# Expert blocks of a decoder layer: down products in two series, the expert's number read once in mid-block

## The chip, the cores and the metric

The kernel runs on one core of a Trainium2 chip. TensorE (PE in the profile) multiplies, VectorE (DVE), ScalarE (ACT) and GpSimd (POOL) work on what it leaves, and SyncE (SP) starts most of the transfers. The metric is the device time of one execution in microseconds (us); less is better.

## What is computed

The program is one decoder layer over 16 sequences of 128 tokens with 256 channels: a two-way recurrent mix, a cross attention, and a causal attention followed by a mixture of eight experts, each with a layer norm behind it. The change lies in the experts alone. Their part of the reference, cut to what matters:

```python
logits = hn @ w_gate.T
probs = jax.nn.softmax(logits, axis=-1)
tv, ti = jax.lax.top_k(probs, TOPK)          # TOPK = 2 of E = 8 experts
tv = tv / jnp.sum(tv, axis=-1, keepdims=True)
rw = jnp.zeros((T, E), hn.dtype).at[jnp.arange(T)[:, None], ti].set(tv)
for e in range(E):                           # FFN = 896, D = 256
    up = jax.nn.silu(hn @ qgroup(w1[e]).T) * (hn @ qgroup(w3[e]).T)
    moe = moe + rw[:, e:e + 1] * (up @ qgroup(w2[e]).T)
```

`qgroup` rounds weights to 16 levels in groups of 128.

## The kernel before

All stages are written out by hand for each engine; order is the order of the code, and semaphores are the only links between the engines. The last large stage, `experts_stage`, takes the 2048 tokens' two choices each, sorted by expert, in 39 blocks of 128 rows. A block belongs to one expert, whose number stands in a table in memory (`k.block_expert`). Three steps are unrolled at the start (`in_steps`), then a loop of 17 turns with two steps each, then two unrolled steps. Buffers come in pairs: `j` is the block's parity, `n` its number.

One block's way through the engines:

1. GpSimd gathers its rows by an indirect DMA (L2211), three bf16 parts of 256 channels.
2. TensorE turns them with six transposes (`turn`, L2062) into a bank of the accumulator memory (PSUM).
3. ScalarE copies the turned rows out into `expert_parts` (`take_rows`, L2125) and raises `parts_ready`. All products of the block read that tile.
4. For each of seven chunks `f` of the 896 hidden channels TensorE makes an up product of twelve bf16 matmuls (`up_product`, L2074) into one of four banks. ScalarE copies half of it out (`first_chunk`, L2130), VectorE adds the other half twice (`second_chunk`, L2168, `gate_ready`), ScalarE takes the silu (`soften`, L2134), and VectorE multiplies (`multiply`, L2175, `up_ready`).
5. For each chunk TensorE adds a down product (`down_product`, L2084): one f32 matmul of 256 columns in the code, which is two matmuls in the trace. A block's down products are made during the step of the next block.
6. ScalarE scales the sum by the tokens' shares (`take_y`, L2140), and GpSimd adds it to the rows in memory by an indirect DMA (`scatter`, L2239).

In a step TensorE reads two expert numbers with `value_load` (L2066), waits for `parts_ready`, and then alternates: up product `f` of this block, down product `f` of the block behind. After the third pair it turns the next block. ScalarE goes through the chunks in a fixed order: copy `f`, then silu `f-1`; the next block's turned rows are copied after the silu that follows copy 4, and the block behind is scaled after the last silu. An up product waits for `gate_ready` of the product four before it (the first two of an odd block: two before), since there are four banks.

Of the kernel before, what the change touches and what calls it, by code (L numbers as in the profile page):

```python
# [38 lines left out]
E, FFN = 8, 896  # L39
FC = FFN // P  # L40
# [7 lines left out]
BLOCKS = (2 * TOK + E * (ROWS - 1)) // ROWS  # L48
# [14 lines left out]
class Steps:  # L63
# [12 lines left out]
    def turn(self, i, per):  # L76
        self.base, self.at = self.start + i * per, 0
# [1905 lines left out]
def experts_stage(k):  # L1983
# [39 lines left out]
    def in_steps(emit, eng, st=None, per=None):  # L2023

        emit(0, 0, 0, False, 2)
        for j in (1, 0):
            emit(j, 2 - j, 0, True, 2)
        if st:
            st.done(1, st.at)
        with eng.Fori(0, TURNS - 2) as i:  # L2030
            if st:
                st.turn(i, per)
            for j in (1, 0):
                emit(j, 2 * i + 4 - j, i + 1, True, 2)
        if st:
            st.done(TURNS - 2, per)
        emit(1, BLOCKS - 2, TURNS - 1, True, 1)
        emit(0, BLOCKS - 1, TURNS - 1, True, 0)

    def bank(j, f):  # L2040

        g = FC * (1 - j) + f
        return UP + g % 4, 2 if g < 2 else 4

    def slot(j, f):

        return (FC * (1 - j) + f) % 2

    def halves(at):
        return banks[:, at, :].rearrange("p (m c s) -> p m c s", m=2, c=DC)  # L2050

    def turned(j):
        return banks.bitcast(BF16)[:, TURN + j, 0:3 * D]
# [4 lines left out]
    def tensor(pe):  # L2058
        def turn(j, n, i):
            pe.wait_ge(rows_in[j], 16 * i + 16)  # L2060
            for a in range(3 * DC):
                last = pe.transpose(turned(j)[:, a * P:(a + 1) * P], rows[j][:, a, :], k.ident16[:, :])  # L2062
            last.then_inc(block_turned, 1)

        def expert_of(n):
            return pe.value_load(k.block_expert[0:1, bass.ds(n, 1)], min_val=0, max_val=E - 1)  # L2066

        def up_product(j, n, f, expert):
            at, before = bank(j, f)
            pe.wait_ge(gate_ready, FC * n + f + 1 + AHEAD - before)  # L2070
            for m in range(2):
                for c in range(DC):
                    for a in range(3):
                        last = pe.matmul(  # L2074
                            banks[:, at, (m * DC + c) * ROWS:(m * DC + c + 1) * ROWS],
                            levels[:, bass.ds(expert * (2 * JOB) + (m * JOB + (f * DC + c) * P), P)],
                            parts[j][:, a, c, :], start=(a == 0), stop=(a == 2))
            last.then_inc(up_summed, 1)

        def down_product(j, n, f, expert):  # L2080
            if f == 0:
                pe.wait_ge(y_ready, n + 1)
            pe.wait_ge(up_ready, FC * n + f + 1)
            last = pe.matmul(banks[:, Y + j, 0:D], up[j][:, f, :], down[:, bass.ds(expert * JOB + f * D, D)],  # L2084
                             start=(f == 0), stop=(f == FC - 1))
            if f == FC - 1:
                last.then_inc(y_summed, 1)

        def step(j, n, i, prev, more):
            expert = expert_of(n)  # L2090
            last_expert = expert_of(n - 1) if prev else None
            pe.wait_ge(parts_ready, n + 1)
            for f in range(FC):
                up_product(j, n, f, expert)
                if prev:
                    down_product(1 - j, n - 1, f, last_expert)
                if more and f == 2:
                    turn(1 - j, n + 1, i + 1 if prev else 0)
            if not prev:
                sum_shares()  # L2100

        def sum_shares():
            for m in range(2):
                pe.wait_ge(shares_hit, m + 1)
                for b in range(B):
                    last = pe.matmul(OF_SHARE, k.row_hit[:, m, b, :], share_hit[:, m, b, :, :].rearrange("p a b -> p (a b)"),
                                     start=(m == 0 and b == 0), stop=(m == 1 and b == B - 1))
            last.then_inc(shares_summed, 1)

        levels = k.levels[:, :, :].rearrange("p m a -> p (m a)")  # L2110
        down = k.down[:, :, :].rearrange("p m a -> p (m a)")
        pe.wait_ge(k.blocks_ready, 1)
        pe.wait_ge(k.bank_read, BANKS_JOB * (NUMBERS + 1))
        pe.wait_ge(k.expert_loads, 16 * (WHOLES + E - LATE))
        turn(0, 0, 0)
        in_steps(step, pe)
        expert = expert_of(BLOCKS - 1)
        for f in range(FC):
            down_product(0, BLOCKS - 1, f, expert)

    def scalar(act):
        def take_rows(j, n):

            act.wait_ge(block_turned, n + 1)
            act.copy(parts[j][:, :, :, :].rearrange("p a c s -> p (a c s)"), turned(j)).then_inc(parts_ready, 1)  # L2125

        def first_chunk(j, n, f):
            act.wait_ge(up_summed, FC * n + f + 1)
            at, _ = bank(j, f)
            act.copy(chunk[slot(j, f)][:, :, :], halves(at)[:, :, 0, :]).then_inc(chunk_ready, 1)  # L2130

        def soften(j, n, f):
            act.wait_ge(gate_ready, FC * n + f + 1 + AHEAD)
            act.activation(silu[slot(j, f)][:, :], gate[slot(j, f)][:, 0, :], ACT.Silu,  # L2134
                           scale=steps[j][:, 0, 0, f:f + 1]).then_inc(silu_ready, 1)

        def take_y(j, n):
            act.wait_ge(y_summed, n + 1)
            act.wait_ge(target_ready, n + 1)
            act.activation(y[j][:, :], banks[:, Y + j, 0:D], ACT.Copy, scale=share[j][:, :]).then_inc(y_ready, 1)  # L2140

        def step(j, n, i, prev, more):
            act.wait_ge(steps_ready, n + 1)
            for f in range(FC):
                first_chunk(j, n, f)
                if f:
                    soften(j, n, f - 1)
                if more and f == 4:
                    take_rows(1 - j, n + 1)
            soften(j, n, FC - 1)  # L2150
            if prev:
                take_y(1 - j, n - 1)

        act.wait_ge(k.tokens_ready, 2)
        act.wait_ge(k.expert_loads, 16 * (WHOLES + E - LATE))
        act.sem_inc(y_ready, 2)
        take_rows(0, 0)
        in_steps(step, act)
        take_y(0, BLOCKS - 1)

# [40 lines left out]
    def gpsimd(pool):  # L2201
# [66 lines left out]
        scatter(0, BLOCKS - 1, TURNS)  # L2268

    return sync, tensor, vector, scalar, gpsimd  # L2270

# [199 lines left out]
```

## Time and profile before

| | us |
|---|---|
| median of 3 runs | 1233.48 (1231.79 to 1234.1) |
| the profiled execution, device time | 1234.32 |
| span of its trace | 1232.6 |
| busy in it: PE, DVE, ACT, POOL | 992.5, 955.7, 747.3, 603.2 |
| expert blocks, first up product to last down product | 860.7 to about 1203.6 |

Times in the trace count from the span's start. The view of line groups gives the number and mean duration of each kind; the timeline gives starts, from which the distance between two operations of one engine is read. A matmul's duration holds its way through the array, so neighbours overlap in it: the distance from start to start is what it costs in a series.

### The profile page before, as it was taken

The numbers are of one execution on the slowest core, as the hardware profiler recorded it, in microseconds if no ns is written. First come the engines' busy times: TensorE is split into PE (matmuls) and PEld (weight loads), VectorE is DVE, ScalarE is ACT, GpSimd is POOL, SyncE is SP. The second block draws the span as 40 slices with busy tenths as digits, with TensorE's granted clock in tenths as the row PEclk, the third lists the DMA queues.
The fourth block names the chain that finished last, engine by engine and source line by source line (L and its number), as shares of the span: only waits on it lengthen the run. The fifth ranks groups of instructions, "written<-read, shape, count | busy, mean of one in ns | idle before, by whom it ended". The sixth has DMA issues, their size and how long they took to land.

```text
span 1232.6 us, 24890 instructions
## 1 busy us (share of the span) xinstructions
PE 992.5 (81%) x7366; PEld 740.9 (60%) x7367; DVE 955.7 (78%) x2172; ACT 747.3 (61%) x1885; POOL 603.2 (49%) x639
## 2 busy tenths in 40 slices
PE   0486866536989998968999999972999999999990
PEld 0342433325767777745566666652888888888880
DVE  6739999997888888737999988746777767776773
ACT  5844434405888888814667776541666666666663
POOL 2839776853444444411566767542434343333333
PEclk9878888867998999968999999995999999999996
DMA  5850010131333333124122222110112121212124
GB/s 200 336 201 0 1 35 0 34 111 57 113 115 121 124 130 132 52 87 199 54 80 69 69 69 69 61 56 24 31 38 39 36 43 32 43 32 43 32 31 145
DMA packets 53493, 96.77 MB, mean 79 GB/s; under 512 B 9840, under 2 KB 41584, under 8 KB 52928
## 3 DMA queue, kind: packets, MB, share of 16 engines
q1 hardware_dynamic: 45328, 83.35, 19.5%
q0 software_dynamic: 8112, 12.78, 5.9%
q8 instruction: 25, 0.41, 0.1%
q14 instruction: 28, 0.23, 0.1%
HBM read 66.37 MB, written 29.74 MB: 78 GB/s over the span
## 4 chain that ended last, share of the span: by engine, by line
PE 45%; DVE 33%; issue 10%; POOL 5%; ACT 3%; DMA 2%; DVEq 0%; ACTq 0%; POOLq 0%; SPq 0%
PE banks L2074 15%; PE banks L2084 10%; DVE mix_sums L651 4%; DVE carry L638 2%; DVE peak L1131 2%; DVE carry L641 2%; DVE whole_stat L234 2%; PE banks L1378 2%; DVE probs L1134 2%; DVE whole_stat L235 2%; PE banks L1356 2%; PE banks L885 1%; PE banks L1393 1%; PE banks L1401 1%; PE banks L911 1%
## 5 line engine op out<-in xcount | busy, mean ns | idle before, releaser
L2168 DVE SCALAR_TENSOR_TENSOR expert_gate<-banks,expert_steps,expert_chunk 128x128 f32<-128x128 f32 x546 | 165.0, 346 | 97.9 <-ACT expert_chunk L2130 90.0
L2074 PE MATMUL banks<-expert_parts,levels 128*128 128x128 bf16 x3276 | 228.5, 220 | 7.1 <-issue 6.0
L2074 PEld LDWEIGHTS banks<-expert_parts,levels 128*128 x3276 | 202.4, 98 | 47.8 <-issue 20.1
L2084 PE MATMUL banks<-down,up 128*128 x546 | 176.2, 406 | 0.0
L2130 ACT COPY expert_chunk<-banks 128x256 f32<-128x256 f32 x273 | 101.7, 373 | 97.7 <-PE banks L2074 94.0
L2239 POOL DMA_INDIRECT summed_d<-expert_y,expert_target x39 | 62.5, 1604 | 178.6 <-ACT expert_y L2140 175.6
L499 PE MATMUL banks<-x_turned,w_rkv 128*128 128x512 f32 (+1 forms) x192 | 101.6, 689 | 39.4 <-DVE weight L632 38.9
L2134 ACT ACTIVATE silu<-expert_gate,expert_steps 128x128 f32<-128x128 f32 x273 | 110.7, 406 | 21.8 <-DVE expert_gate L2168 19.8
L1100 POOL TENSOR_TENSOR whole<-whole_level,whole_stat 128x896 bf16<-128x896 f32 x32 | 53.3, 1686 | 101.6 <-DVE whole_level L1171 101.6
L2175 DVE SCALAR_TENSOR_TENSOR up<-expert_gate,expert_steps,silu 128x128 f32<-128x128 f32 x273 | 94.8, 347 | 8.2 <-ACT silu L2134 8.2
L499 PEld LDWEIGHTS banks<-x_turned,w_rkv 128*128 128x128 f32 x192 | 41.7, 223 | 97.0 <-issue 96.0
L1028 ACT ACTIVATE whole_level<-whole_raw,whole_stat 128x128 f32<-128x128 f32 x224 | 91.3, 486 | 0.2 <-DVE whole_stat L255 0.2
L2084 PEld LDWEIGHTS banks<-down,up 128*128 128x128 f32 x546 | 83.0, 191 | 0.4
L923 PE MATMUL banks<-v_ones,probs_t 128*128 128x17 f32 x512 | 63.4, 266 | 0.0
L923 PEld LDWEIGHTS banks<-v_ones,probs_t 128*128 128x128 f32 x512 | 62.0, 198 | 0.0
L550 ACT ACTIVATE weight<-weight 128x1024 f32<-128x1024 f32 x16 | 16.9, 1058 | 71.9 <-DVE weight L632 71.9
L393 PE MATMUL banks<-consts,level 128*128 128x128 f32 x84 | 19.5, 424 | 50.6 <-POOL level L376 50.6
L1356 PE MATMUL banks<-attend_w,xn_t 128*128 128x512 f32 x128 | 59.2, 606 | 0.0
L1401 PE MATMUL banks<-attend_w,o_turn 128*128 128x256 f32 x256 | 58.1, 380 | 0.5 <-ACT logits L1515 0.5
L1494 ACT ACTIVATE att_probs<-att_probs,low_peak 128x128 f32<-128x128 f32 x128 | 49.6, 393 | 11.4 <-DVE low_peak L1737 11.3
L2211 POOL DMA_INDIRECT expert_rows<-normed_d,token x39 | 39.8, 1019 | 31.3 <-POOL token L2208 30.5
L651 DVE RECIPROCAL mix_sums<-gate 128x512 f32<-128x512 f32 x16 | 53.7, 3353 | 0.6
(265 smaller groups left out, 2483.2 us busy)
## 6 DMA issues: line engine op xcount, KB each, us to landing
whole_raw<-in_weight_jobs SPq DMA_DIRECT2D x16, 896.0 KB, 5.1
levels_d<-whole_t SPq DMA_DIRECT2D x16, 448.0 KB, 2.8
levels<-levels_d SPq DMA_DIRECT2D x16, 448.0 KB, 3.5
raw<-in_weight_jobs SPq DMA_DIRECT2D x6, 896.0 KB, 4.7
numbers_d<-turned SPq DMA_DIRECT2D x6, 896.0 KB, 6.4
down<-in_weight_jobs SPq DMA_DIRECT2D x5, 896.0 KB, 5.5
normed_d<-normed_parts SPq DMA_DIRECT2D x16, 192.0 KB, 1.8
attend_w<-numbers_d SPq DMA_DIRECT2D x3, 896.0 KB, 6.4
```

The costliest lines, as they stand in the source:

```text
L499: last = pe.matmul(banks[:, 3 * (u % 2) + m, :], w_rkv[:, kc, col:col + P], x_turned[d][:, kc, bass.ds(g * GT, GT)], start=(kc == 0), stop ...
L651: st.did(dve.reciprocal(sums[p][:, 1, :], gate[u][:, :]))
L923: last = pe.matmul(banks[:, HEADS, head * (XK + 1):(head + 1) * (XK + 1)], probs_t[h][:, 4 * m + a, :], v_ones[j][:, head, :], start=True, ...
L1028: last = act.activation(level[j][:, a, :], raw[j][:, a, :], ACT.Identity, bias=stat[j][:, BIAS, a:a + 1], scale=stat[j][:, INV, a:a + 1])
L1356: last = pe.matmul(banks[:, Q + m, :], xn_t[:, c, :], w_qkv[:, c, 512 * m:512 * m + 512], start=(c == 0), stop=(c == DC - 1))
L1401: last = pe.matmul(banks[:, TURN, 0:D], o_turn[:, h, :], w_o[:, h, :], start=(h == 0), stop=(h == QH - 1))
L2074: last = pe.matmul(banks[:, at, (m * DC + c) * ROWS:(m * DC + c + 1) * ROWS], levels[:, bass.ds(expert * (2 * JOB) + (m * JOB + (f * DC + ...
L2084: last = pe.matmul(banks[:, Y + j, 0:D], up[j][:, f, :], down[:, bass.ds(expert * JOB + f * D, D)], start=(f == 0), stop=(f == FC - 1))
L2130: act.copy(chunk[slot(j, f)][:, :, :], halves(at)[:, :, 0, :]).then_inc(chunk_ready, 1)
L2134: act.activation(silu[slot(j, f)][:, :], gate[slot(j, f)][:, 0, :], ACT.Silu, scale=steps[j][:, 0, 0, f:f + 1]).then_inc(silu_ready, 1)
L2168: last = dve.scalar_tensor_tensor(out=gate[slot(j, f)][:, m, :], in0=halves(at)[:, m, 1, :], scalar=steps[j][:, m, 1, f:f + 1], in1=chunk[ ...
L2175: dve.scalar_tensor_tensor(out=up[j][:, f, :], in0=gate[slot(j, f)][:, 1, :], scalar=steps[j][:, 1, 0, f:f + 1], in1=silu[slot(j, f)][:, : ...
```

## The change

Four things move, and no arithmetic changes.

- TensorE's step makes down products 0 to 3 of the block behind first, then up products 0 to 3, then down products 4 to 6, the turn of the next block, and up products 4 to 6.
- The expert's number is loaded into one of two held registers, once for each block, right behind the turn; a step only takes the register's value. Before, each step loaded two numbers at its start.
- ScalarE scales the block behind (`take_y`) after the silu that follows copy 4, not after the last silu.
- ScalarE copies the next block's turned rows (`take_rows`) one chunk later, after the silu that follows copy 5.

```diff
--- before.py
+++ after.py
@@ -2062,8 +2062,13 @@
                 last = pe.transpose(turned(j)[:, a * P:(a + 1) * P], rows[j][:, a, :], k.ident16[:, :])
             last.then_inc(block_turned, 1)
 
-        def expert_of(n):
-            return pe.value_load(k.block_expert[0:1, bass.ds(n, 1)], min_val=0, max_val=E - 1)
+        expert_held = [pe.alloc_register(f"expert_{j}") for j in range(2)]
+
+        def load_expert(j, n):
+            pe.reg_load(expert_held[j], k.block_expert[0:1, bass.ds(n, 1)])
+
+        def expert_of(j):
+            return pe.snap(expert_held[j], min_val=0, max_val=E - 1)
 
         def up_product(j, n, f, expert):
             at, before = bank(j, f)
@@ -2086,16 +2091,21 @@
             if f == FC - 1:
                 last.then_inc(y_summed, 1)
 
+        DOWN_RUN = 4
+
         def step(j, n, i, prev, more):
-            expert = expert_of(n)
-            last_expert = expert_of(n - 1) if prev else None
+            expert = expert_of(j)
+            last_expert = expert_of(1 - j) if prev else None
             pe.wait_ge(parts_ready, n + 1)
             for f in range(FC):
+                if prev and f in (0, DOWN_RUN):
+                    for d in range(f, DOWN_RUN if f == 0 else FC):
+                        down_product(1 - j, n - 1, d, last_expert)
+                if more and f == DOWN_RUN:
+                    turn(1 - j, n + 1, i + 1 if prev else 0)
+                if more and f == DOWN_RUN:
+                    load_expert(1 - j, n + 1)
                 up_product(j, n, f, expert)
-                if prev:
-                    down_product(1 - j, n - 1, f, last_expert)
-                if more and f == 2:
-                    turn(1 - j, n + 1, i + 1 if prev else 0)
             if not prev:
                 sum_shares()
 
@@ -2112,9 +2122,10 @@
         pe.wait_ge(k.blocks_ready, 1)
         pe.wait_ge(k.bank_read, BANKS_JOB * (NUMBERS + 1))
         pe.wait_ge(k.expert_loads, 16 * (WHOLES + E - LATE))
+        load_expert(0, 0)
         turn(0, 0, 0)
         in_steps(step, pe)
-        expert = expert_of(BLOCKS - 1)
+        expert = expert_of(0)
         for f in range(FC):
             down_product(0, BLOCKS - 1, f, expert)
 
@@ -2145,11 +2156,11 @@
                 first_chunk(j, n, f)
                 if f:
                     soften(j, n, f - 1)
-                if more and f == 4:
+                if prev and f == 4:
+                    take_y(1 - j, n - 1)
+                if more and f == 5:
                     take_rows(1 - j, n + 1)
             soften(j, n, FC - 1)
-            if prev:
-                take_y(1 - j, n - 1)
 
         act.wait_ge(k.tokens_ready, 2)
         act.wait_ge(k.expert_loads, 16 * (WHOLES + E - LATE))
```

TensorE at the start of the loop. In names, `up0` is the even block's product buffer and `expert_parts1` the odd block's turned rows; a line with ISA or REGISTER_ALU sets a register. Before:

```order
L2066 TENSOR_LOAD block_expert
L2066 ISA x3
L2066 TENSOR_LOAD block_expert
L2066 ISA x2
L2092 REGISTER_ALU
L2070 ISA [waits expert_parts_ready]
L2074 ISA [waits gate_ready]
L2074 MATMUL banks<-expert_parts1,levels 128x128 x3
```

After (L2087 to L2089 are the down product, L2079 the up product):

```order
L2087 REGISTER_ALU [waits expert_parts_ready]
L2088 ISA [waits y_ready]
L2089 ISA [waits up_ready]
L2089 MATMUL banks<-down,up0 128x256
L2088 REGISTER_ALU
L2089 ISA [waits up_ready]
L2089 MATMUL banks<-down,up0 128x256
```

The two loads are gone from here. The wait for the turned rows stands ahead of the four down products, which don't read them.

ScalarE in the same turn of the loop, from the copy of chunk 4 of the odd block (`expert_chunk0`) on. Before:

```order
L2130 COPY expert_chunk0<-banks 128x256 [waits up_summed]
L2133 REGISTER_ALU
L2134 ACTIVATE silu1<-expert_gate1,expert_steps1 128x128 [waits gate_ready]
L2124 REGISTER_ALU
L2125 COPY expert_parts0<-banks 128x768 [waits block_turned]
L2130 COPY expert_chunk1<-banks 128x256 [waits up_summed]
L2133 REGISTER_ALU
L2134 ACTIVATE silu0<-expert_gate0,expert_steps1 128x128 [waits gate_ready]
```

After:

```order
L2141 COPY expert_chunk0<-banks 128x256 [waits up_summed]
L2144 REGISTER_ALU
L2145 ACTIVATE silu1<-expert_gate1,expert_steps1 128x128 [waits gate_ready]
L2151 ACTIVATE expert_y0<-banks,expert_share0 128x256 [waits target_ready,y_summed]
L2141 COPY expert_chunk1<-banks 128x256 [waits up_summed]
L2144 REGISTER_ALU
L2145 ACTIVATE silu0<-expert_gate0,expert_steps1 128x128 [waits gate_ready]
L2135 REGISTER_ALU
L2136 COPY expert_parts0<-banks 128x768 [waits block_turned]
```

Between copy 4 with its silu and the copy of the turned rows three operations have come: the scaling, copy 5, and silu 4, which waits for VectorE.

## Rows read from the trace of the kernel before

**Rows 1.** Page, part 4: the chain that ended last, by line, shares of the span.

```profile
PE banks L2074 15%; PE banks L2084 10%; DVE mix_sums L651 4%; DVE carry L638 2%; DVE peak L1131 2%; DVE carry L641 2%; DVE whole_stat L234 2%; PE banks L1378 2%; DVE probs L1134 2%; DVE whole_stat L235 2%; PE banks L1356 2%; PE banks L885 1%; PE banks L1393 1%; PE banks L1401 1%; PE banks L911 1%
```

**Rows 2.** Windows: stretch, length, busy us of PE, PEld, DVE, ACT, POOL, clock, DMA.

```profile
900.00:1000.00 100.00, 97.94 (x1190) 84.08 (x1188) 69.81 (x239) 65.32 (x184) 38.76 (x71) 1.00 0.22 39
```

**Rows 3.** Timeline of PE, two blocks: start, us, engine, line, names, count.

```profile
1009.33 0.84 PE L2074 MATMUL banks<-expert_parts,levels 128*128 128x128 bf16 x12 [0.34 <-issue]
...
1012.81 0.50 PE L2062 MATMUL banks<-ident,expert_rows 128*128 128x128 bf16 x6
...
1013.15 0.83 PE L2074 MATMUL banks<-expert_parts,levels 128*128 128x128 bf16 x12
...
1014.30 0.83 PE L2074 MATMUL banks<-expert_parts,levels 128*128 128x128 bf16 x12
...
1014.97 0.65 PE L2084 MATMUL banks<-down,up 128*128 x2
...
1015.46 0.83 PE L2074 MATMUL banks<-expert_parts,levels 128*128 128x128 bf16 x12
...
1017.87 0.84 PE L2074 MATMUL banks<-expert_parts,levels 128*128 128x128 bf16 x12
...
1025.82 0.65 PE L2084 MATMUL banks<-down,up 128*128 x2
...
1026.82 0.84 PE L2074 MATMUL banks<-expert_parts,levels 128*128 128x128 bf16 x12 [0.34 <-issue]
```

**Rows 4.** Timeline: products in series, in the first block and after the last.

```profile
864.65 2.84 PE L2074 MATMUL banks<-expert_parts,levels 128*128 128x128 bf16 x48
...
1199.91 3.67 PE L2084 MATMUL banks<-down,up 128*128 x16
```

**Rows 5.** One line's instructions on PE's sequencer (PEldq): ns min/median/max.

```profile
L2066 PEldq TENSOR_LOAD <-block_expert x78: 296/299/493, 858.9 to 1198.7; - x78
...
L2030 PEldq COMPARE_BRANCH  x17: 83/215/215, 902.3 to 1182.2; - x17
...
L2092 PEldq ALU_OP  x1: 36/36/36, 1026.5 to 1026.5; - x1
```

**Rows 6.** Timeline of ACT, same two blocks.

```profile
1009.89 0.46 ACT L2140 ACTIVATE expert_y<-banks,expert_share 128x256 f32<-128x256 f32 x1
...
1010.25 0.36 ACT L2130 COPY expert_chunk<-banks 128x256 f32<-128x256 f32 x1
...
1014.02 0.37 ACT L2130 COPY expert_chunk<-banks 128x256 f32<-128x256 f32 x1 [0.68 <-PE banks L2074]
...
1015.39 0.37 ACT L2130 COPY expert_chunk<-banks 128x256 f32<-128x256 f32 x1 [0.70 <-PE banks L2074]
...
1015.66 0.40 ACT L2134 ACTIVATE silu<-expert_gate,expert_steps 128x128 f32<-128x128 f32 x1
...
1015.96 0.79 ACT L2125 COPY expert_parts<-banks 128x768 bf16<-128x768 bf16 x1
```

**Rows 7.** Timeline of DVE, same two blocks.

```profile
1014.42 0.61 DVE L2168 SCALAR_TENSOR_TENSOR expert_gate<-banks,expert_steps,expert_chunk 128x128 f32<-128x128 f32 x2 [0.48 <-ACT expert_chunk L2130]
```

**Rows 8.** Timeline of ACT and POOL at the stage's end.

```profile
1201.54 0.46 ACT L2140 ACTIVATE expert_y<-banks,expert_share 128x256 f32<-128x256 f32 x1
...
1202.80 1.57 POOL L2239 DMA_INDIRECT summed_d<-expert_y,expert_target  x1 [3.34 <-ACT expert_y L2140]
...
1207.35 1.55 POOL L2239 DMA_INDIRECT summed_d<-expert_y,expert_target  x1 [2.98 <-DMA summed_d<-expert_y,expert_target]
```

**Rows 9.** Timeline and windows: the first block, clock down at its start; the attention.

```profile
859.75 0.80 ACT L2125 COPY expert_parts<-banks 128x768 bf16<-128x768 bf16 x1 [8.69 <-PE banks L2062]
...
860.69 3.79 PE L2074 MATMUL banks<-expert_parts,levels 128*128 128x128 bf16 x36 [0.98 <-ACT expert_parts L2125]
...
628.18 0.44 PE L1407 MATMUL banks<-consts,normed 128*128 128x128 f32 x2 [1.26 <-DVE normed L1753]
...
625.00:665.00 40.00, 36.23 (x180) 24.37 (x180) 36.85 (x91) 27.17 (x84) 26.81 (x29) 1.00 0.16 53
```

## The prediction, made before the changed kernel had run

> **What bounds the kernel now.** First the page's chain that ended last: the up products' line alone holds 15% of the span and the down products' 10%, more than any other two [rows 1]. The change touches only this stage, so next the windows: in 100 us of it TensorE is busy for 97.94 us, VectorE for 69.81, ScalarE for 65.32, at full clock (1.00, the 2.4 GHz level) [rows 2]. The stage runs at TensorE's pace, and the other two have room. The third view is TensorE's timeline [rows 3]. Two steps take 1026.82 - 1009.33 = 17.49 us, so 8.745 each. Inside, an up product takes 0.67 us from start to start (1014.30 to 1014.97), a down product 0.49 (to 1015.46), the turn 0.34 (1012.81 to 1013.15). Seven pairs and a turn are 7 x 1.16 + 0.34 = 8.46. The rest stands at the boundaries: two pairs after 1015.46 the next step is due at 1017.78 and comes at 1017.87, 0.09 late; the down product of 1025.82 ends its 0.49 at 1026.31 and the loop's next turn comes at 1026.82, 0.51 late. Mean 0.30.
>
> **Part 1, down products in series.** Before, each stands alone, at 0.49. Behind the last block they stand in series, sixteen matmuls of which the last has 0.43 of its own: 3.67 us, less about 0.43, over 15 distances is 0.216, so 0.43 for a product of two [rows 4]. The 0.055 more is what the step from an f32 to a bf16 product costs. There were seven such steps in a block, now two: 5 x 0.055 = 0.28 us less. Up products in series keep 0.67: 48 matmuls in 2.84 us [rows 4].
>
> **Part 2, the expert's number.** At a boundary the sequencer ran two loads of 0.30 us each and, in the loop, a branch of 0.22 [rows 5]. That is what made it late by 0.09 and 0.51. One load is left, behind three down products and a turn (1.30 + 0.06 + 0.34 = 1.7 us of TensorE's queue), and it hides there; the snaps are short. I take the whole 0.30 as gone; if the single load showed whole, it would be 0.30 back. Without anything else a step would be 8.745 - 0.28 - 0.30 = 8.17 us.
>
> **Part 3, the order on ScalarE, which I think decides.** Call the start of up product 4 U. In the new step four down products, a change, four up products, three down products, a change and the turn go ahead of it: 1.73 + 0.055 + 2.68 + 1.30 + 0.055 + 0.335 = 6.15 us. Behind it stand three up products, 2.01 us, and then the next step's first instruction waits for the turned rows. When are they there? Along ScalarE [rows 6]:
> - copy 4 starts 0.87 after its product's start (product 1013.15, copy 1014.02), at times 1.09 (1014.30, 1015.39): U + 0.87;
> - silu 3 follows 0.27 behind (1015.39 to 1015.66): U + 1.14. Its gate is long made;
> - the scaling, which now stands here, 0.30 behind (distance from a silu to what follows, 1015.66 to 1015.96): U + 1.44;
> - copy 5 0.36 behind it (1009.89 to 1010.25): U + 1.80. Its product was ready for it at U + 0.67 + 0.87, earlier;
> - silu 4 0.27 behind: U + 2.07. Its gate: VectorE starts 0.40 after copy 4 and takes 0.61 (1014.02, 1014.42) [rows 6, 7], so U + 1.88, in time;
> - the rows' copy 0.30 behind, at U + 2.37, lasting 0.79: U + 3.16.
>
> TensorE then needs a restart, since the sequencer itself waited: from the register instruction (1026.5) to the matmul (1026.82) there are 0.3 us [rows 3, 5]; I take 0.38, the 0.08 being my allowance for the semaphore and a down product's larger weight load. So the next step starts at U + 3.54 where it could start at U + 2.01: a stall of 1.53 us. Before, the same copy began at 1015.96 and ended at 1016.75, 1.1 us ahead of the step at 1017.87 [rows 3, 6]: the slack was there because the turn was made three pairs earlier and the copy stood right behind silu 3.
>
> Queued behind the waiting instruction are the four down products, which don't need the rows and could have filled 1.73 us. They can't pass it. Who waits for that: ScalarE and VectorE, for the next up product, and both have room.
>
> A step is then 6.15 + 3.54 = 9.69 us, 0.945 more than 8.745.
>
> **Other waits.** Up products of a burst come 0.67 apart while VectorE, busy 69.81 us in 100 [rows 2], needs some 6.1 us for a step's seven chunks, 0.87 each; but the fifth comes 1.7 us after the fourth's end, so the backlog is gone by U. Down products 0 to 3 need silus made before U + 1.5. The scaling also waits for its last down product, made before the turn, and for a copy of the shares on GpSimd, which has until 7.6 us into the step. I cost these three at nothing: the three down products, the turn and 2 us of up products cover them.
>
> **The end.** Before, block 37 is scaled after block 38's last silu (1201.54), its scatter starts at 1202.80, and the last scatter (1207.35) waits for its landing [rows 8]. Now block 37 is scaled at U + 1.44, 0.57 before the last up product's end; its scatter starts 1.26 behind that, at +0.69, and the last scatter 4.55 behind it, at +5.24 (block 38's own sum, seven down products and a scaling later, is there before). In the old order the last scatter came at 1207.35 - 1199.91 = +7.44 [rows 4, 8]. Gain 2.2.
>
> **The sum.** 37 steps (blocks 1 to 37) at +0.945: +35.0. Block 38's step has no stall behind it: -0.3. The end: -2.2. Block 0: its turn moves too, but 32 other matmuls stand behind it and cover the wait: 0. Together +32.5 on the profiled 1234.32 (the span of 1232.6 and 1.7 around it, which stays) is 1266.8. The runs' median is 0.8 lower, so **1266 us, slower by 2.6%**. Bounds: copy 4 at 1.09 instead of 0.87 in all steps adds 37 x 0.22 = 8; a restart of 0.14, as in the first block (copy from 859.75 for 0.80, matmul at 860.69 [rows 9]), takes 37 x 0.24 = 9 off; a load that shows whole adds 11.
>
> **Rivals.**
> - *The rows come in time.* If ScalarE got to the rows' copy 1.5 us earlier than my row-by-row order says, the parts 1 and 2 would be all: 1234.3 - 38 x 0.28 - 37 x 0.30 - 2.2 = 1210.4, 1210 by the median. It decides at a rows' copy that starts before U + 0.84. The room of both engines [rows 2] speaks for it; against it speaks that the copy stands behind copy 5, and up product 5 ends only at U + 1.54 in ScalarE's eyes. Even with every engine free the stall would be 1.54 + 0.27 + 0.30 + 0.79 + 0.38 - 2.01 = 1.27. Chance 0.09.
> - *Half a stall*, 0.6 us, where gain and loss meet, within 0.2% (about what a measurement of this kernel can tell from no change): 0.03, for the same reason.
> - *The clock falls.* TensorE now rests 1.5 us in each step. With the clock at its lower level (1.2 GHz) three up products took 3.79 us, some 1.2 each without the last one's drain [rows 9], so a step at that level would cost 7 x 0.53 + 7 x 0.43 = 6.7 us more; if one step in seven ran so, 37 / 7 x 6.7 = +35, 1301. Against it: a rest of 1.26 us at 628.18 lies in a stretch whose clock is 1.00 [rows 9]. No row shows a rest that returns every 10 us. The Trainium skill, TensorE: Matmul & The Clock Gate, section "A second HAM failure mode: psum-queue depth-cycling", says that small idles between groups of matmuls which rotate through banks can make the clock swing between its levels; by that rule this rival comes true, and the row on the single rest speaks against it. Chance 0.06.
> - *The load in mid-block is no longer hidden*, or ScalarE is later still (the scaling waits for GpSimd): 37 x 0.3 to 0.5, 1277 to 1284. Chance 0.06.
>
> **How the numbers follow.** The forecast, 1255 to 1276, has 0.76. The range runs from 1253 to 1284, which takes in the later-still case; it leaves out the rows in time and the fallen clock. Slower: 0.76 + 0.06 + 0.06 = 0.88; same 0.03; faster 0.09.
>
> **What the changed profile would show.** Two steps from first down product to first down product in 19.4 us (17.49 before), not 16.3. Down products in series of eight and six matmuls at 0.43 a product. TensorE idle about 1.4 us (the stall less the last matmul's drain, which counts as busy) ahead of the first down product, put down to the copy of the turned rows, some 37 times, together 50 to 60 us where now there is 1 such wait. ScalarE: scaling, copy 5, silu 4 and the rows' copy in a row without a gap. The wait of GpSimd's scatter moves earlier. I am wrong if the rows' copy ends before up product 6 does, or if the stall is there and the clock in the stage is below 1.00.

## The result, and the profile after

The changed kernel takes 1265.5 us (median of 4 runs, 1258.5 to 1266.4), the kernel before 1232.6 (1228.0 to 1234.1): ratio 1.026, 95% interval 1.0215 to 1.0307. It is slower, and the range of the prediction (1253 to 1284, likeliest 1266) holds it. The profiled execution took 1266.19 us against 1234.32 before, 31.9 more. One execution of run 1 below took 3411.8 us, where its nine others took 1222.6 to 1230.5, and is left out of that run's ratio.

TensorE's timeline of two steps, where it answers to [rows 3]:

```profile
1010.12 2.17 PE L2079 MATMUL banks<-expert_parts,levels 128*128 128x128 bf16 x36
1013.51 1.99 PE L2089 MATMUL banks<-down,up 128*128 x8 [1.22 <-ACT expert_parts L2136]
1015.34 2.84 PE L2079 MATMUL banks<-expert_parts,levels 128*128 128x128 bf16 x48
1018.01 1.51 PE L2089 MATMUL banks<-down,up 128*128 x6
1019.37 0.50 PE L2062 MATMUL banks<-ident,expert_rows 128*128 128x128 bf16 x6
1019.70 2.17 PE L2079 MATMUL banks<-expert_parts,levels 128*128 128x128 bf16 x36
1023.25 1.99 PE L2089 MATMUL banks<-down,up 128*128 x8 [1.37 <-ACT expert_parts L2136]
```

The down products stand in series of eight and six matmuls, the up products in fours and threes. Ahead of each series of eight there is a gap, [1.22] and [1.37] us, and it is put down to the copy of the turned rows (L2136, once L2125). The distance from the start of up product 4 (1010.12) to the next step (1013.51) is 3.39 us, in the loop's other half 1019.70 to 1023.25, 3.55.

ScalarE in the first of the two, where it answers to [rows 6]:

```profile
1010.99 0.37 ACT L2141 COPY expert_chunk<-banks 128x256 f32<-128x256 f32 x1 [1.25 <-PE banks L2079]
1011.26 0.40 ACT L2145 ACTIVATE silu<-expert_gate,expert_steps 128x128 f32<-128x128 f32 x1
1011.56 0.47 ACT L2151 ACTIVATE expert_y<-banks,expert_share 128x256 f32<-128x256 f32 x1
1011.92 0.37 ACT L2141 COPY expert_chunk<-banks 128x256 f32<-128x256 f32 x1
1012.17 0.42 ACT L2145 ACTIVATE silu<-expert_gate,expert_steps 128x128 f32<-128x128 f32 x1
1012.48 0.80 ACT L2136 COPY expert_parts<-banks 128x768 bf16<-128x768 bf16 x1
```

From U = 1010.12: copy 4 at +0.87, silu 3 at +1.14, scaling at +1.44, copy 5 at +1.80, silu 4 at +2.05, rows' copy at +2.36, ending at +3.16. From copy 4 on ScalarE has no gap in these rows; it is TensorE that stands.

The waits of the stage, the windows and the group of the down products (the columns are those of the views before):

```profile
PE banks L2089 <- ACT expert_parts L2136: 47.0, 37, 1.4
```

```profile
1000.00:1100.00 100.00, 86.25 (x1084) 78.83 (x1081) 64.34 (x219) 59.66 (x168) 32.97 (x61) 1.00 0.18 33
```

```profile
L2089 PE MATMUL banks<-down,up 128*128 x546 | 136.5, 390 | 47.0 <-ACT expert_parts L2136 47.0
```

37 waits of up to 1.4 us, 47.0 us together (50 to 60 were expected), where before one wait for this copy stood in the whole trace, 1.0 us in the first block. TensorE is busy for 86 us of 100, not 98 as in [rows 2], and the clock stays at 1.00. VectorE and ScalarE did less in the same 100 us as well: they were supplied less, not short of room.

### The profile page after: what moved, and what is told of

It reads as the page before. It is cut to its first block, busy times and chain, and to the rows that moved or that the text cites. A ratio compares the mean times of both kernels' runs of the same rounds, so it can differ in the third digit from the quotient of the medians.

```text
span 1264.3 us, 24713 instructions
## 1 busy us (share of the span) xinstructions
PE 985.6 (78%) x7366; PEld 752.8 (60%) x7367; DVE 956.7 (76%) x2172; ACT 747.7 (59%) x1885; POOL 598.1 (47%) x639
## 4 chain that ended last, share of the span: by engine, by line
PE 39%; DVE 33%; issue 12%; ACT 8%; POOL 5%; DMA 2%; DVEq 0%; ACTq 0%; POOLq 0%; SPq 0%
PE banks L2079 11%; PE banks L2089 10%; DVE mix_sums L651 4%; ACT expert_parts L2136 2%; DVE carry L638 2%; DVE whole_stat L235 2%; DVE peak L1131 2%; DVE carry L641 2%; DVE whole_stat L234 2%; PE banks L1378 2%; ACT silu L2145 2%; DVE probs L1134 2%; PE banks L1356 2%; PE banks L1393 1%; PE banks L1401 1%
## 5 line engine op out<-in xcount | busy, mean ns | idle before, releaser
L2179 DVE SCALAR_TENSOR_TENSOR expert_gate<-banks,expert_steps,expert_chunk 128x128 f32<-128x128 f32 x546 | 166.4, 347 | 130.9 <-ACT expert_chunk L2141 114.0
L2079 PE MATMUL banks<-expert_parts,levels 128*128 128x128 bf16 x3276 | 197.4, 220 | 1.0 <-ACT expert_parts L2136 1.0
L2079 PEld LDWEIGHTS banks<-expert_parts,levels 128*128 x3276 | 189.5, 98 | 6.8 <-issue 1.2
L2089 PE MATMUL banks<-down,up 128*128 x546 | 136.5, 390 | 47.0 <-ACT expert_parts L2136 47.0
L2089 PEld LDWEIGHTS banks<-down,up 128*128 128x128 f32 x546 | 97.4, 190 | 63.9 <-issue 53.9
L2186 DVE SCALAR_TENSOR_TENSOR up<-expert_gate,expert_steps,silu 128x128 f32<-128x128 f32 x273 | 95.1, 348 | 8.2 <-ACT silu L2145 8.2
```

Source lines behind the costliest of these rows:

```text
L2079: last = pe.matmul(banks[:, at, (m * DC + c) * ROWS:(m * DC + c + 1) * ROWS], levels[:, bass.ds(expert * (2 * JOB) + (m * JOB + (f * DC + ...
L2179: last = dve.scalar_tensor_tensor(out=gate[slot(j, f)][:, m, :], in0=halves(at)[:, m, 1, :], scalar=steps[j][:, m, 1, f:f + 1], in1=chunk[ ...
L2186: dve.scalar_tensor_tensor(out=up[j][:, f, :], in0=gate[slot(j, f)][:, 1, :], scalar=steps[j][:, 1, 0, f:f + 1], in1=silu[slot(j, f)][:, : ...
```

## The experiments

The quantity that tells most is the length of a step: the mean distance of first up products over 32 steps in the middle of the stage. It was 8.749 us before and 9.648 after. The stages ahead of this one start the first up product anywhere from 852.5 to 860.7 us in these traces, so single times scatter by a few microseconds for reasons that don't concern the change; the step doesn't. Every ratio below is to the kernel before, run on the same chip. The runs come from several chips, and the kernel before took 1228.3 to 1232.8 us on them, so times of different runs are compared by their ratios and not by their microseconds. Where an expectation gives a time only, the step in the table is worked out from it.

The theory: the chain on ScalarE from copy 4 to the rows' copy sets the start of the next step, since the wait stands ahead of down products that don't need it. The rivals: the series themselves, a busy ScalarE or VectorE, or the clock.

| kernel | step, us | step expected | time, us | ratio (95%) |
|---|---|---|---|---|
| before | 8.749 | | 1232.6 | |
| after | 9.648 | 9.69 | 1265.5 | 1.026 (1.0215 to 1.0307) |
| 1 rows first | 8.717 | 8.76 | 1229.0 | 0.9985 (0.9959 to 1.001) |
| 2 wait late | 8.158 | 8.17 | 1205.9 | 0.978 (0.974 to 0.982) |
| 3 scaling last | 9.490 | 9.54 | 1259.3 | 1.0255 (1.022 to 1.029) |
| 4 register only | 8.437 | 8.45 | 1221.3 | 0.991 (0.989 to 0.994) |
| 5 late wait, loads at start | 9.073 | 8.5 or 8.8 | 1243.4 | 1.011 (1.006 to 1.015) |
| 6 rows first and wait late | 8.266 | 8.17 | 1212.8 | 0.987 (0.983 to 0.991) |
| 7 all seven down products in a series | 9.976 | 8.3 to 8.4 | 1273.1 | 1.037 (1.032 to 1.042) |
| 8 rows later | 10.706 | 10.47 | 1304.1 | 1.058 (1.0535 to 1.062) |
| 9 late wait, one load at start | 8.261 | 8.16 | 1212.6 | 0.985 (0.9815 to 0.988) |
| 10 wait late, again | 8.158 | 8.16 | 1209.1 | 0.982 (0.979 to 0.985) |
| 11 series alone | 9.287 | 9.07 | 1249.3 | 1.015 (1.011 to 1.018) |

### 1. The rows' copy first

```diff
-                if prev and f == 4:
-                    take_y(1 - j, n - 1)
-                if more and f == 5:
+                if more and f == 4:
                     take_rows(1 - j, n + 1)
+                if prev and f == 4:
+                    take_y(1 - j, n - 1)
```

> The changed kernel, but ScalarE copies the next block's turned rows right behind silu 3, and scales the block behind after that. Theory (the chain of ScalarE's operations ahead of the rows' copy sets the start of the next step): the copy starts at U + 1.44 (U: start of up product 4), lasts 0.79, restart 0.38, so the next step starts at U + 2.61 instead of U + 3.54. A step takes 8.76 us, TensorE idles 0.6 us a step, and the kernel comes to about 1232 us, the time before the change. Rival (the series of products themselves or the banks slow the stage, the wait for the rows only shows it): the gap stays above 1 us and the time above 1255.

The step is 8.717 us, 0.93 less than after, by moving three ScalarE operations past the rows' copy and nothing else. TensorE's waits for the rows shrink:

```profile
1014.71 1.99 PE L2089 MATMUL banks<-down,up 128*128 x8 [0.29 <-ACT expert_parts L2136]
...
1023.47 1.99 PE L2089 MATMUL banks<-down,up 128*128 x8 [0.40 <-ACT expert_parts L2136]
```

0.29 and 0.40 us are left; the 0.6 of the expectation held the last matmul's drain, about 0.16, too. Over the 32 steps the rows' copy now ends at U + 2.23 instead of U + 3.16, which is 0.93 earlier as well. The rival fell: the series are as they were in the changed kernel, and the stage is back at its old pace.

### 2. The wait behind the down products

```diff
-            pe.wait_ge(parts_ready, n + 1)
             for f in range(FC):
                 if prev and f in (0, DOWN_RUN):
                     ...
+                if f == 0:
+                    pe.wait_ge(parts_ready, n + 1)
```

> The changed kernel, but TensorE waits for the turned rows ahead of up product 0, behind the four down products, which don't read them. ScalarE's order is that of the change. Theory: rows are there at U + 3.2, up product 0 is due at U + 2.01 + 1.73 = U + 3.74, so nothing waits; a step takes 8.17 us, two steps 16.3, and the kernel about 1210 us. Rival (the wait only moves behind the down products, since ScalarE or VectorE is the bound once the stage is packed): idle time of 0.5 us or more ahead of up product 0, 1225 us or more.

```profile
1014.79 1.95 PE L2089 MATMUL banks<-down,up 128*128 x8
...
1022.95 1.95 PE L2089 MATMUL banks<-down,up 128*128 x8
...
1027.41 1.51 PE L2089 MATMUL banks<-down,up 128*128 x6
```

No gap stands ahead of the series of eight, and two of them are 1022.95 - 1014.79 = 8.16 us apart. That is what TensorE's work alone takes (4.69 + 3.02 + 0.11 + 0.34 = 8.16, by the prediction's rows). ScalarE's order is the slow one, the rows' copy still ends at U + 3.16 on the mean, and now it costs nothing. This kernel beats both, by 2.2% the one before; in a second session (10) by 1.8%.

> The kernel with the late wait once more, in more rounds. Step 8.16 us; ratio to the kernel before 0.975 to 0.985.

### 3 and 8. The length of ScalarE's chain, shorter and longer

```diff
-                if prev and f == 4:
-                    take_y(1 - j, n - 1)
                 if more and f == 5:
                     take_rows(1 - j, n + 1)
             soften(j, n, FC - 1)
+            if prev:
+                take_y(1 - j, n - 1)
```

> The changed kernel, with the scaling of the block behind back at the step's end, behind the last silu. Theory: copy 5 then starts at U + 1.54 instead of 1.80, but silu 4 waits for gate 4 until U + 1.92, so the rows' copy starts at U + 2.22 instead of 2.37: 0.15 less a step, -5.5 us, and the end loses its 2.2 us: about 1262 us. Rival (the scaling is the whole delay): 0.36 less a step, 1255.

The step fell by 0.158 us, where 0.15 was expected and the rival said 0.36. Copy 5, silu 4 and the rows' copy, with U = 1012.50:

```profile
1014.04 0.37 ACT L2141 COPY expert_chunk<-banks 128x256 f32<-128x256 f32 x1
1014.42 0.40 ACT L2145 ACTIVATE silu<-expert_gate,expert_steps 128x128 f32<-128x128 f32 x1
1014.73 0.78 ACT L2136 COPY expert_parts<-banks 128x768 bf16<-128x768 bf16 x1
```

Copy 5 starts at +1.54, 0.26 earlier, but silu 4 follows it by 0.38 instead of 0.25 us: with the scaling away it waits for VectorE's gate instead. The ratio, 1.0255 against 1.026, can't tell so small a gain from none; it is the step that shows it.

Run 8 makes the chain longer, from the changed kernel:

```diff
-                if more and f == 5:
+                if more and f == 6:
                     take_rows(1 - j, n + 1)
```

> The changed kernel, with the copy of the turned rows one chunk later still, behind silu 5. Theory: silu 5 waits for gate 5 (copy 5 at U + 1.80, gate made at U + 2.81), so the rows' copy starts at U + 3.15 instead of U + 2.37: each step 0.78 us longer, 37 x 0.78 = 29, about 1294 us. Rival (some other thing holds the next step, and the copy has room left): less than 10 us more.

The trace, then two windows:

```profile
967.23 1.99 PE L2089 MATMUL banks<-down,up 128*128 x8 [2.06 <-DVE up L2186]
...
977.75 1.99 PE L2089 MATMUL banks<-down,up 128*128 x8 [2.16 <-DVE up L2186]
...
988.17 1.99 PE L2089 MATMUL banks<-down,up 128*128 x8 [2.05 <-DVE up L2186]
990.00 2.84 PE L2079 MATMUL banks<-expert_parts,levels 128*128 128x128 bf16 x48
...
998.75 2.43 PE L2089 MATMUL banks<-down,up 128*128 x8 [2.21 <-DVE up L2186]
1000.97 4.09 PE L2079 MATMUL banks<-expert_parts,levels 128*128 128x128 bf16 x48
...
1010.81 1.99 PE L2089 MATMUL banks<-down,up 128*128 x8 [2.06 <-DVE up L2186]
```

```profile
950.00:1000.00 50.00, 39.35 (x487) 35.95 (x485) 30.25 (x103) 27.91 (x79) 15.00 (x27) 1.00 0.17 30
1000.00:1050.00 50.00, 41.56 (x508) 38.06 (x507) 28.14 (x96) 26.03 (x74) 14.39 (x27) 0.97 0.17 32
```

The view names VectorE's multiply (L2186) ahead of these gaps, since that ended last. It is not what held TensorE: the down products behind the gap read chunks 0 to 3, which were multiplied long before, and the rows' copy ends 0.23 us ahead of the series of 988.17, as in the changed kernel:

```profile
987.16 0.78 ACT L2136 COPY expert_parts<-banks 128x768 bf16<-128x768 bf16 x1
```

Most steps are as expected: 977.75 - 967.23 = 10.52 and 988.17 - 977.75 = 10.42. But the one from 998.75 takes 12.06: its down products 2.43 us instead of 1.99, its four up products 4.09 instead of 2.84, and the granted clock of that stretch is 0.97, not 1.00. The rest ahead of it was 2.21 us. The trace's record of the clock has six falls to the lower level in this stage, from 880.7, 925.1, 1000.2, 1085.5, 1160.6 and 1235.7 us on; in none of the twelve other traces does the clock fall between the stage's first products and its last. So the rival of the falling clock is real where TensorE rests 2.1 to 2.2 us in each step (at 10 to 11 us a step), and it accounts for the part of the step that the chain doesn't (10.706 against 10.47), and so for most of the 10 us by which the time, 1304 us, passed the expected 1294. The changed kernel's own rests, up to 1.4 us, show none of it. Rests between 1.4 and 2.1 us were not tried.

### 4 and 11. One part alone, from the kernel before

Run 4 has the kernel before with the held register, loaded behind the turn at `f == 2`; 11 has it with the down products' order alone.

```diff
-            expert = expert_of(n)
-            last_expert = expert_of(n - 1) if prev else None
+            expert = expert_of(j)
+            last_expert = expert_of(1 - j) if prev else None
...
                 if more and f == 2:
                     turn(1 - j, n + 1, i + 1 if prev else 0)
+                if more and f == 2:
+                    load_expert(1 - j, n + 1)
```

> The kernel before, with the expert's number alone changed: one load for a block, behind the turn, into a held register; down products one by one, ScalarE's order as before. Theory: the boundary's 0.09 and 0.51 us, mean 0.30, were the two loads on the sequencer; they go, 37 x 0.30 = 11 us, so about 1222 us and two steps in 16.9 us. Rival (the loop's branch, not the loads, makes the 0.51): only some 3 to 5 us go, 1228.

0.312 us a step, the prediction's 0.30. The branch alone makes no lateness: both boundaries are gone, and steps of about 8.5 and 8.95 us, which alternated before, are all 8.44.

```diff
             for f in range(FC):
+                if prev and f in (0, DOWN_RUN):
+                    for d in range(f, DOWN_RUN if f == 0 else FC):
+                        down_product(1 - j, n - 1, d, last_expert)
                 up_product(j, n, f, expert)
-                if prev:
-                    down_product(1 - j, n - 1, f, last_expert)
```

> The kernel before with the down products' order alone changed: series of four and three; turn, wait, loads and ScalarE's order as before. By the prediction's price for the series (0.28 a step less): 1223 us. Theory now: the rows are ready at U + 2.3, and the sequencer is only 1.0 us ahead after three up products in series, so the two loads show with 0.67 and 1.15 us at the boundaries, as they did with the loads at the start: step 9.07 us, 12 us more than before, about 1243.

The prediction's price for the series, -0.28 us, does not hold for it alone: the step grows by 0.54.

```profile
1014.47 2.17 PE L2074 MATMUL banks<-expert_parts,levels 128*128 128x128 bf16 x36
1017.84 1.99 PE L2084 MATMUL banks<-down,up 128*128 x8 [1.19 <-issue]
...
1024.03 2.17 PE L2074 MATMUL banks<-expert_parts,levels 128*128 128x128 bf16 x36
1026.84 1.99 PE L2084 MATMUL banks<-down,up 128*128 x8 [0.64 <-ACT expert_parts L2128]
```

The gaps are 1.19 and 0.64 us, the larger one at the loop's branch. The second is put down to the rows' copy, but in both cases that copy had ended (1016.70 and 1026.26) before the second load's register work did (1017.33 and 1026.38): it is the loads that make the gaps, in the way that runs 5 and 9 show below. My number for the step was 0.22 too small. It came from run 5; here TensorE's sequencer takes 2.25 us from the branch to the first matmul, where it takes 2.00 in run 5, since the wait for the rows and one more instruction stand there too. That is most of the rest at the branch; the other boundary was not worked out.

### 5 and 9. Loads at the boundary, with the late wait

Both stand on run 2. Run 5 puts the two `value_load`s back at the step's start; run 9 loads one number there. Run 5:

```diff
-            expert = expert_of(j)
-            last_expert = expert_of(1 - j) if prev else None
+            expert = expert_of(n)
+            last_expert = expert_of(n - 1) if prev else None
...
-                if more and f == DOWN_RUN:
-                    load_expert(1 - j, n + 1)
```

and run 9:

```diff
+            if prev:
+                load_expert(j, n)
             expert = expert_of(j)
...
-                if more and f == DOWN_RUN:
-                    load_expert(1 - j, n + 1)
```

> The wait for the turned rows stands behind the four down products, and the expert's numbers are again loaded twice at a step's start. Theory of the prediction (the boundary's loads cost what they cost before, 0.30 us a step): 1210 + 11 = 1221 us. Rival, from the changed kernel's trace: three up products in series leave TensorE's sequencer only about 1.0 us ahead, and the two loads take 1.4 us, with the branch 1.7, so 0.4 to 0.8 us show: about 1232.

> As the kernel with the late wait, but the block's own expert number is loaded once at the step's start instead of in mid-block. The run with two loads at the start showed that the sequencer reaches the boundary about 1.0 us ahead of TensorE's last up product, and that a load with its following register instruction costs some 0.4 to 0.65 us there, the branch 0.35. Theory (what counts is the sum on the sequencer against a lead of 1.0 us): one load of 0.36 plus the branch of 0.35 in every second step plus 0.2 of register moves stays under 1.0, so nothing shows: step 8.16 us, the time of the late wait alone. Rival (any load at the boundary shows whole): 0.36 a step, 13 us more.

In run 5 the step is 0.92 us longer than with the load in mid-block: not 0.30, and more than the 0.4 to 0.8 of the rival too. The view names a multiply again (L2179), of chunks that the down products behind the gap don't read. When does the sequencer reach the loop's branch? The row of the branch in three kernels (before, run 5, run 9), in a window with one boundary each:

```profile
L2030 PEldq COMPARE_BRANCH  x1: 215/215/215, 1024.7 to 1024.7; - x1
```

```profile
L2030 PEldq COMPARE_BRANCH  x1: 215/215/215, 1010.6 to 1010.6; - x1
```

```profile
L2030 PEldq COMPARE_BRANCH  x1: 207/207/207, 1014.4 to 1014.4; - x1
```

and TensorE's rows beside it in run 5 and in run 9:

```profile
1009.53 2.17 PE L2074 MATMUL banks<-expert_parts,levels 128*128 128x128 bf16 x36
1012.65 1.99 PE L2084 MATMUL banks<-down,up 128*128 x8 [0.94 <-DVE up L2179]
...
1018.84 2.17 PE L2074 MATMUL banks<-expert_parts,levels 128*128 128x128 bf16 x36
1021.48 1.99 PE L2084 MATMUL banks<-down,up 128*128 x8 [0.47 <-DVE up L2179]
```

```profile
1013.28 2.17 PE L2079 MATMUL banks<-expert_parts,levels 128*128 128x128 bf16 x36
1015.46 1.99 PE L2089 MATMUL banks<-down,up 128*128 x8
...
1021.65 2.17 PE L2079 MATMUL banks<-expert_parts,levels 128*128 128x128 bf16 x36
1023.66 1.95 PE L2089 MATMUL banks<-down,up 128*128 x8
```

Before, the branch ran at 1024.7 while the next step was due at 1026.31: 1.6 us ahead. In run 5 it ran at 1010.6, and the step was due at 1009.53 + 2.01 = 1011.54: 0.9 ahead. In matmuls that is the same lead. Before, one of down product 5 (the first had started at 1024.67), twelve of up product 6 and two of down product 6 were still to start, 15. In run 5, 21 of the 36 had started, since (1010.65 - 1009.53) / 0.056 is 20 distances, so 15 again; in run 9 the same (1014.4 against 1013.28). Counted by start times it is 15 at all 17 branches of each of the three traces; in run 7, where products wait for VectorE, it is only 5 or 6. Where nothing else holds it, the sequencer leads by a number of matmuls, and dense bf16 products make it short in time. What it has to do from the branch to the next matmul, less that lead, is the lateness: before, 2.14 - 1.63 = 0.51 us, which is what [rows 3] show; in run 5, 2.00 - 0.89 = 1.11, and the series starts at 1012.65 instead of 1011.54. That is why two loads, which showed 0.30 us a step between alternating products, show 0.92 behind three up products in series. Run 9 bears it out: one load shows 0.17 us where the branch is also run (1015.46 against 1015.29 due) and nothing where it isn't (1023.66 against 1023.66). The expectation had it stay hidden in both places; the step is 0.10 us longer than expected, because the register work at the branch came to 1.05 us against a lead of 0.89.

### 6 and 7. Both mends, and one long series

> Both mends: the wait for the turned rows behind the four down products, and ScalarE's copy of the rows ahead of the scaling. Theory: with the wait late the rows have room already, so the second mend adds nothing: within 2 us of the kernel with the late wait alone (about 1210).

Run 6 has the edits of 1 and 2 together. The step is 0.11 longer than in 2 alone: steps of 8.16 and about 8.4 alternate. The copy of the rows now stands ahead of copies 5 and 6, and an odd block's first up products wait for the last gates of the block before (their banks are two products old, not four). The rows that show it, up products 0 to 3 of an odd block and of the even one behind it:

```profile
1015.17 3.03 PE L2079 MATMUL banks<-expert_parts,levels 128*128 128x128 bf16 x48
...
1023.52 2.84 PE L2079 MATMUL banks<-expert_parts,levels 128*128 128x128 bf16 x48
```

3.03 us in the odd block, 2.84 in the even one. In the odd block up product 1 was due at 1015.84 and started at 1016.02; the gate of chunk 6 of the block before had ended at 1015.88. So the order on ScalarE in the changed kernel is the better one, once the wait stands late.

Run 7 has the edits of 1 and 2 and makes all seven down products at the step's start:

```diff
-                if prev and f in (0, DOWN_RUN):
-                    for d in range(f, DOWN_RUN if f == 0 else FC):
+                if prev and f == 0:
+                    for d in range(FC):
                         down_product(1 - j, n - 1, d, last_expert)
...
-                if more and f == DOWN_RUN:
+                if more and f == 4:
                     turn(1 - j, n + 1, i + 1 if prev else 0)
-                if more and f == DOWN_RUN:
+                if more and f == 4:
                     load_expert(1 - j, n + 1)
```

> As the one with both mends, but all seven down products in one series at the step's start. One change from f32 to bf16 fewer: 38 x 0.055 = 2 us less. But down product 6 is due at U + 2.01 + 6 x 0.43 = U + 4.6, and its multiply ends at about U + 4.85 by ScalarE's and VectorE's rows. Theory: a wait of some 0.3 us ahead of it in each step eats the gain, 5 to 10 us more than with both mends. Rival (VectorE is early enough): 2 us less.

This expectation was far off: 9.976 us a step, not 8.3 to 8.4. TensorE waits ahead of down product 4 and again ahead of 5:

```profile
1010.52 0.69 PE L2089 MATMUL banks<-down,up 128*128 x2 [0.72 <-DVE up L2187]
1011.51 1.26 PE L2089 MATMUL banks<-down,up 128*128 x4 [0.29 <-DVE up L2187]
```

VectorE's rows, in the next step the gates of chunks 2 to 4 (L2180), show why:

```profile
1016.04 0.61 DVE L2180 SCALAR_TENSOR_TENSOR expert_gate<-banks,expert_steps,expert_chunk 128x128 f32<-128x128 f32 x2
...
1017.03 0.61 DVE L2180 SCALAR_TENSOR_TENSOR expert_gate<-banks,expert_steps,expert_chunk 128x128 f32<-128x128 f32 x2
...
1018.02 0.61 DVE L2180 SCALAR_TENSOR_TENSOR expert_gate<-banks,expert_steps,expert_chunk 128x128 f32<-128x128 f32 x2
```

Supplied without a pause, the two engines need 0.99 us a chunk (1016.04, 1017.03, 1018.02), more than the 0.87 that I took from busy time: each silu waits for a gate, and each gate for the copy that stands behind the silu before on ScalarE. Chunk 5's gate came 1.41 us after chunk 4's (1019.44), since the rows' copy and the scaling stand ahead of its copy. Seven chunks then outlast the 5.0 us of up products and turn, the last down products wait for their multiplies, and the next block's up products wait behind them, so the blocks no longer overlap. With series of four and three, the first four chunks are worked off while TensorE makes three down products and the turn.

## Why the prediction was right, point by point

- **The chain on ScalarE** was right operation by operation: +0.87, 1.14, 1.44, 1.80, 2.05, 2.36, 3.16 against +0.87, 1.14, 1.44, 1.80, 2.07, 2.37, 3.16. Runs 1, 3 and 8 show that it sets the step. The rows' copy ends at U + 3.16 in the changed kernel and at U + 2.23, 3.01 and 4.00 in these three, by the mean of the 32 steps. Shortened by 0.93, the chain makes the step fall by 0.93; by 0.15, by 0.16; lengthened by 0.84 (0.78 was expected), it makes two steps at full clock (10.52 and 10.42) 0.82 longer on the mean.
- **The restart** was taken as 0.38 us. It was 0.36 at the loop's head on the mean, but 0.23 in the middle of a turn, where two register instructions stand between the rows' copy and the matmul and not three. The mean of both is 0.30, 0.08 less than taken; the part up to U took 6.19 and not 6.15. So the step was 9.648 and not 9.69.
- **The place of the wait**, ahead of down products that don't need it, was the second half of the cause: run 2 moves it alone and gains 1.49 us a step.
- **The sum** came out 0.7 us too large in the span (+31.8, where +32.5 was in it), and that close by luck in part, since terms missed in both directions. The 37 steps from block 1's start to block 38's grew by 33.9 us (356.5 against 322.6), where +35.0 was in the sum. Block 0 got 0.35 shorter, where 0 was taken. Block 38's step, up to the last up product's end, got 0.25 longer (7.87 against 7.62), where -0.3 was taken: down product 6 of the block behind stood behind that end before, and now it stands ahead of it. Behind it 1.6 us were gained, not 2.2: the last scatter started 5.76 us after the last up product's end (1239.05 against 1233.29), where 5.24 was expected and 7.44 stood before, because the landing of the scatter before it took longer:

```profile
1234.00 1.57 POOL L2250 DMA_INDIRECT summed_d<-expert_y,expert_target  x1 [4.98 <-ACT expert_y L2151]
1239.05 1.55 POOL L2250 DMA_INDIRECT summed_d<-expert_y,expert_target  x1 [3.48 <-DMA summed_d<-expert_y,expert_target]
```

  With 0.4 us less ahead of the stage that makes the measured 31.8 us of span.
- **Part 2, the load, was right in the sum; its price holds for one order only.** Its price of 0.30 holds between alternating products (run 4, 0.31). In the new order the same loads would cost 0.92 (run 5). In the same way part 1's -0.28 can't be had alone (run 11, +0.54); with the loads away it is there in full (8.437 in run 4, 8.158 in run 2). Taken together the two give 0.59, where the sum had 0.58 (run 2). The sum came out right because the change makes both.
- **"Other waits"** cost nothing, as said: in the changed kernel's trace the waits for the rows' copy are the only ones of TensorE from 875 to 1230 us. But the figure for VectorE in it, 0.87 us a chunk from its busy share, was too low; 0.99 is what a series takes (run 7). With a pause behind the fourth up product it made no difference.
- **The clock** stayed at 1.00 in the changed kernel, as the likeliest case had it. The rival was no empty one, though: run 8's rests of 2.1 to 2.2 us brought it about. What the section "A second HAM failure mode: psum-queue depth-cycling" of TensorE: Matmul & The Clock Gate in the Trainium skill says, that small idles between groups of matmuls can make the clock swing, agrees with run 8 (granted clock 0.97) and did not come true at the changed kernel's rests of up to 1.4 us.

## What to carry to other kernels

Before an operation is moved down an in-order engine, add up what now stands ahead of it against what the consumer has left to do; and put a wait right ahead of the first instruction that needs it, since everything between is held too. A gain that is read from rows between alternating operations belongs to that mixture: series of dense products shorten the sequencer's lead in time, so that register loads and branches which hid before come out. The busy share of two engines that hand work to and fro understates what a chunk takes when it is supplied without pause.

## What the runs showed of the hardware that was not expected

- TensorE's sequencer ran 15 matmuls ahead, each with its weight load, at boundaries of different density (before, runs 5 and 9): 1.6 us where f32 down products stood among them, 0.9 us where all were bf16. The Trainium skill, TensorE: Matmul & The Clock Gate, table at the top, gives a queue of 64 for the engine. 15 matmuls and their weight loads make 30, so the measured lead is less than half of that.
- Rests of 2.1 to 2.2 us that return every 10.5 us came with falls of the clock to its lower level in some steps (run 8: six falls in the stage, one step of 12.06 us among ones of 10.4 to 10.5). Rests of up to 1.4 us every 9.6 us came with none in the whole stage.
